# Tail of a decoder layer: TensorE transposes of the attention output replaced by transposing DMAs out of half-precision halves

## The reference, cut to what matters

```python
x = _layernorm(x + self_attention(x))                      # 16 batches of 112 tokens, D = 256
q, k, v = x @ Wq, ctx @ Wk, ctx @ Wv                       # 8 heads of 128; all 6000 keys seen by all 1792 tokens
out = softmax(1.5 * (q k^T) * DIM_HEAD ** -0.5 ...) @ v    # per head
x = _layernorm(x + out.reshape(1792, 1024) @ Wout + bout)
h = gelu(x @ ternary(W1).T + b1)                           # 1024 hidden
x = _layernorm(x + h @ ternary(W2).T + b2)
```

## Time and profile before

| | us |
|---|---|
| median of three runs | 2306.89 |
| the profiled execution | 2306.85 |
| its span in the profile | 2305.1 |
| around the span | 1.75 |

### The profile page before, as it was taken

The page is one execution under the profiler, slowest core; times in us unless marked ns, Lnnn a source line. Parts: engine busy times, 40 slices in busy tenths (PEclk is TensorE's granted clock), DMA queues, the critical chain, the costliest instruction groups (busy, mean ns, idle before and its releaser), DMA issues.

```text
span 2305.1 us, 61948 instructions
## 1 busy us (share of the span) xinstructions
PE 2252.5 (98%) x26078; PEld 1980.7 (86%) x26078; DVE 2020.4 (88%) x2241; ACT 1865.1 (81%) x2224; POOL 1898.6 (82%) x1153
## 2 busy tenths in 40 slices
PE   7998999999999999999999999999999999999998
PEld 4557998899889998899888998899889998998886
DVE  7878988988889888988898898988899888898876
ACT  4357888888888888888878888888888888888855
POOL 8675888888878888888888898888878888899953
PEclk8999999999999999999999999999999999999999
DMA  7400000000000000000000000000000000010220
GB/s 201 158 32 21 6 4 13 4 7 6 11 6 4 7 13 4 6 4 7 13 4 5 6 13 4 6 4 7 13 4 6 4 6 6 4 47 7 90 79 33
DMA packets 34837, 50.44 MB, mean 22 GB/s; under 512 B 2304, under 2 KB 27392, under 8 KB 34560
## 3 DMA queue, kind: packets, MB, share of 16 engines
q1 hardware_dynamic: 34560, 46.46, 6.5%
HBM read 30.99 MB, written 15.47 MB: 20 GB/s over the span
## 4 chain that ended last, share of the span: by engine, by line
PE 71%; POOL 15%; DVE 6%; issue 4%; ACT 3%; POOLq 0%; DVEq 0%; ACTq 0%
PE psum L420 26%; POOL e_lo L1618 12%; PE psum L452 9%; PE psum L445 9%; PE psum L450 5%; PE psum L448 5%; PE psum L567 4%; PE psum L557 4%; POOL e_hi L1612 3%; DVE run_max L1082 3%; ACT ring L847 2%; PE psum L693 2%; PE psum L740 1%; PE psum L529 1%; PE psum L574 1%
## 5 line engine op out<-in xcount | busy, mean ns | idle before, releaser
L1618 POOL TENSOR_TENSOR e_lo<-ring,e_hi 128x1024 f16<-128x1024 f32 (+1 forms) x665 | 1388.8, 2103 | 196.4 <-ACT ring L862 160.8
L1082 DVE TENSOR_TENSOR run_max<-psum,run_max 128x1024 f16<-128x1024 f32 (+1 forms) x616 | 737.9, 1198 | 183.5 <-ACT ring L847 180.3
L847 ACT ACTIVATE ring<-psum 128x1024 f32<-128x1024 f32 (+1 forms) x672 | 673.7, 1003 | 180.0 <-PE psum L420 104.8
L1103 DVE SCALAR_TENSOR_TENSOR ring<-ring,psum 128x1024 f32<-128x1024 f32 (+1 forms) x672 | 792.5, 1186 | 0.7 <-PE psum L660 0.7
L420 PE MATMUL psum<-qx_hi,k_hi 128*128 128x256 f16 x2632 | 718.0, 273 | 15.5 <-DVE run_max L1082 9.1
L420 PE MATMUL psum<-qx_hi,k_lo 128*128 128x256 f16 x2632 | 717.8, 273 | 0.0
L420 PE MATMUL psum<-qx_lo,k_hi 128*128 128x256 f16 x2632 | 717.7, 273 | 0.0
L452 PE MATMUL psum<-v_main,e_lo 128*128 128x129 f16 x4032 | 711.4, 220 | 0.0
L862 ACT ACTIVATE ring<-ring 128x1024 f32<-128x1024 f32 (+1 forms) x672 | 696.1, 1036 | 1.3 <-DVE ring L1103 0.7
L445 PE MATMUL psum<-v_main,e_hi 128*128 128x257 f16 x2016 | 550.4, 273 | 1.3 <-POOL e_lo L1618 1.3
L450 PE MATMUL psum<-v_main,e_hi 128*128 128x128 f16 x2016 | 446.9, 222 | 0.0
(11 more groups left out here) (203 smaller groups left out, 3171.2 us busy)
## 6 DMA issues: line engine op xcount, KB each, us to landing
o_scratch<-o_buf SPq DMA_DIRECT2D x56, 128.0 KB, 1.9
raw<-o_scratch SPq DMA_DIRECT2D x14, 512.0 KB, 4.4
stage<-in_ctxT SPq DMA_DIRECT2D x6, 500.0 KB, 3.9
stage<-in_ctxT SPq DMA_DIRECT2D x12, 250.0 KB, 4.9
w_scratch<-wall SPq DMA_DIRECT2D x1, 2304.0 KB, 10.9
wall<-w_scratch SPq DMA_DIRECT2D x6, 384.0 KB, 3.2
x<-in_xT SPq DMA_DIRECT2D x4, 448.0 KB, 6.6
res<-in_x SPq DMA_DIRECT2D x1, 1792.0 KB, 17.6
```

Source lines behind the costliest of these rows:

```text
L847: a.activation(ring[:, f % SLOTS, 0:n], pair(f)[:, 0:n], ACT.Copy).then_inc(s_kept, 1)
L1082: ins = v.tensor_tensor(run_max[:, 0:n], pair(f)[:, 0:n], run_max[:, 0:n], ALU.max)
L1103: v.scalar_tensor_tensor(slot, slot, LIFT, psum[:, 6, 0:QB].unsqueeze(1).broadcast_to([P, t, QB]), ALU.add, ALU.subtract).then_inc(s_sub, 1)
L1618: g.tensor_tensor(e_lo[f % NEL][:, 0:n], slot, e_hi[f % NEH][:, 0:n], ALU.subtract).then_inc(s_lo, 1)
```

## The change

A returned tile is no longer transposed by TensorE. ScalarE copies it from `raw` (SBUF) as float16 into the high part of `halved`, VectorE subtracts into the low part beside it (two buffers), and a transposing DMA on SyncE's queue (`turn_tile`) turns the 128 x 2048 float16 values (512 KB) into `oT`, which holds six tiles; TensorE's projection reads its operands there. `o_high(i)` waits for the load and, from tile 2 on, for the DMA of tile i - 2; `turn_tile(i)` waits for `o_low(i)` and, from tile 6 on, for the projection of tile i - 6. Eight tiles instead of five are split during the last groups, at every second turn from turn -1. The turns of the projections stay. The pairs of tiles 6 to 13 are projected into banks 6, 0, 1 and 6 instead of bank 6 alone, since banks 0 and 1 no longer receive transposes. On SyncE's queue the loads are spread out between the transposing DMAs.

```diff
-        O_TURN = {3 * i: i for i in range(5)}
+        O_TURN = {2 * i - 1: i for i in range(8)}
-        oT_hi = [at(KREG + 14336 + 2048 * r, f"oT_hi{r}", [P, NH, P], F16) for r in range(2)]
-        oT_lo = [at(KREG + 18432 + 2048 * r, f"oT_lo{r}", [P, NH, P], F16) for r in range(2)]
+        halved = [at(KREG + 14336 + 4096 * r, f"halved{r}", [P, NH, 2, DH], F16) for r in range(2)]
+        NOT = 6
+        oT = [at(CTX + 10240 + 4096 * r, f"oT{r}", [P, NH, 2, P], F16) for r in range(NOT)]
+        s_oT = [sem(f"t_turned{r}") for r in range(NOT)]
...
-            return (7, 3, 2)[p] if p < 3 else 6
+            return (7, 3, 2)[p] if p < 3 else (6, 0, 1)[p % 3]
-            return 6 if p == 5 else 7
+            return 0 if p == 5 else 7
...
-                def o_transposes(i):
...
                 def o_project(i, heads=range(NH)):
-                        pe.wait_ge(t_lo, i + 1)
+                        pe.wait_ge(s_oT[i % NOT], 16 * (i // NOT + 1))
...
+                        elif i == 2:
+                            pe.wait_ge(s_max, NF_ALL)
                         elif i == 6:
                             pe.wait_ge(s_sub, NF_ALL)
-                        elif i % 2 == 0 and p >= 4:
-                            pe.wait_ge(t_add, p)
+                        elif i == 12:
+                            pe.wait_ge(t_add, 4)
...
                 def o_high(i):
-                    a.wait_ge(t_tr, i + 1)
+                    a.wait_ge(s_raw[i % NRAW], 16 * (i // NRAW + 1))
                     if i >= 2:
-                        a.wait_ge(t_wp, i - 1)
-                    a.activation(oT_hi[i % 2]..., psum[:, 0:2, :], ACT.Copy).then_inc(t_hi, 1)
+                        a.wait_ge(s_oT[(i - 2) % NOT], 16 * ((i - 2) // NOT + 1))
+                    a.activation(halved[i % 2][:, :, 0, :], raw[i % NRAW][:, :, :], ACT.Copy).then_inc(t_hi, 1)
                 def o_low(i):
-                    v.tensor_tensor(oT_lo[i % 2]..., psum[:, 0:2, :], oT_hi[i % 2]..., ALU.subtract)
+                    v.tensor_tensor(halved[i % 2][:, :, 1, :], raw[i % NRAW][:, :, :], halved[i % 2][:, :, 0, :],
+                                    ALU.subtract).then_inc(t_lo, 1)
...
+                def turn_tile(i):
+                    sp.wait_ge(t_lo, i + 1)
+                    if i >= NOT:
+                        sp.wait_ge(t_wp, i - NOT + 1)
+                    sp.dma_start_transpose(oT[i % NOT][:, :, :, :].rearrange("p h x t -> p (h x) t"),
+                                           halved[i % 2][:, :, :, :].rearrange("p h x d -> p (h x d)")).then_inc(
+                                               s_oT[i % NOT], 16)
...
                     if n == NBLK - 3:
                         sp.wait_ge(s_lo, LATE)
-                        for i in range(3, 6):
+                        for i in range(3, 5):
                             load_tile(i)
+                        for i in range(3):
+                            turn_tile(i)
+                            load_tile(i + 5)
                     if n == NBLK - 2:
-                        for i in range(6, 10):
-                            load_tile(i)
-                for i in range(10, NTL):
-                    load_tile(i)
+                        for i in range(3, 7):
+                            turn_tile(i)
+                            load_tile(i + 5)
+                for i in range(7, NTL):
+                    if i + 5 < NTL:
+                        load_tile(i + 5)
+                    turn_tile(i)
```

More of the change, by code:

```diff
@@ L389, in columns @@
             return (FIRST[c + 1] - FIRST[c]) * P
-        (t_bias, t_tr, t_hi, t_lo, t_wp, t_n, t_cp, t_n3, t_add, t_nt, t_yh, t_yl, t_f1, t_ge, t_hh, t_hl, t_f2, t_add2,
+        (t_bias, t_hi, t_lo, t_wp, t_n, t_cp, t_n3, t_add, t_nt, t_yh, t_yl, t_f1, t_ge, t_hh, t_hl, t_f2, t_add2,
          t_bn, t_bn2, t_ag, t_sq, t_ag3, t_sq3, t_shift,
          t_n3a, t_last, t_out) = [
-            sem("t_" + n) for n in ("bias", "tr", "hi", "lo", "wp", "n", "cp", "n3", "add", "nt", "yh", "yl", "f1", "ge",
+            sem("t_" + n) for n in ("bias", "hi", "lo", "wp", "n", "cp", "n3", "add", "nt", "yh", "yl", "f1", "ge",
                                     "hh", "hl", "f2", "add2", "bn", "bn2", "ag", "sq", "ag3", "sq3", "shift", "n3a", "last",
@@ L684, in o_project @@
                             pe.wait_ge(s_late, 48)
+                        elif i == 2:
+                            pe.wait_ge(s_max, NF_ALL)
                         elif i == 6:
                             pe.wait_ge(s_sub, NF_ALL)
-                        elif i % 2 == 0 and p >= 4:
-                            pe.wait_ge(t_add, p)
+                        elif i == 12:
+                            pe.wait_ge(t_add, 4)
                     for h in heads:
-                        for n, (o, w) in enumerate(((oT_hi, wout_hi), (oT_hi, wout_lo), (oT_lo, wout_hi))):
+                        for n, (o, w) in enumerate(((0, wout_hi), (0, wout_lo), (1, wout_hi))):
                             mm = pe.matmul(psum[:, bank_of_projection(p), (i % 2) * D:(i % 2 + 1) * D],
-                                           lhsT=o[i % 2][:, h, :], rhs=w[:, h, :],
+                                           lhsT=oT[i % NOT][:, h, o, :], rhs=w[:, h, :],
                                            start=(h == 0 and n == 0), stop=(h == NH - 1 and n == 2))
@@ L770, in step @@
                         o_project(*O_PROJECT[turn])
-                    if turn in O_TURN:
-                        o_transposes(O_TURN[turn])
                 def blocks(first, last, past=0):
@@ L796, in _ @@
                 blocks((NH - 2) * NQB, NBLK)
-                o_transposes(5)
                 o_project(4)
-                o_transposes(6)
                 n_transposes(0)
                 o_project(5)
-                o_transposes(7)
                 n_transposes(1)
@@ L808, in _ @@
                     up(c, range(0, 4))
-                    o_transposes(i)
                     o_project(i - 1)
                     up(c, range(4, 8))
-                    o_transposes(i + 1)
                     o_project(i)
                     down(2 * c)
-                    if c == 0:
-                        o_transposes(i + 2)
                     n_transposes(2 * c + 2)
@@ L821, in _ @@
                         n_transposes(3)
-                        o_transposes(i + 3)
                         o_project(i + 2)
@@ L1032, in _ @@
                 a.wait_ge(s_bias, 16)
-                o_high(5)
                 second_root(0)
-                o_high(6)
                 n_high(0)
-                o_high(7)
                 n_high(1)
@@ L1437, in _ @@
                             inverse(3)
-                    if f - TAIL - 1 in O_TURN:
-                        o_low(O_TURN[f - TAIL - 1])
+                    if f - TAIL in O_TURN:
+                        o_low(O_TURN[f - TAIL])
                 first_residual(0)
@@ L1444, in _ @@
                 second_statistics(0)
-                o_low(5)
                 second_norms(0)
-                o_low(6)
                 n_low(0)
                 first_residual(2)
-                o_low(7)
                 n_low(1)
@@ L1676, in load_tile @@
                     if i >= NRAW:
-                        sp.wait_ge(t_tr, i - NRAW + 1)
+                        sp.wait_ge(t_lo, i - NRAW + 1)
                     sp.dma_start(raw[i % NRAW][:, :, :].rearrange("p h d -> p (h d)"),
                                  o_part[i * P:(i + 1) * P, :]).then_inc(s_raw[i % NRAW], 16)
+                def turn_tile(i):
[5 more added lines that the diff above has]
+                                               s_oT[i % NOT], 16)
                 for n in range(NBLK):
```

4 lines of the change are left out of this document (removed).

## The result

The changed kernel takes 2320.28 us in the median of four runs (2318.50 to 2320.63), the kernel before 2306.57 beside it: ratio 1.0057, 95% interval 1.0045 to 1.0070. By the ratio it is slower by 13.2 us (by the two medians 13.7) where 3.3 us gained were forecast; the time lies inside the range, near its upper end, but the side was wrong. The profiled execution after took 2318.50, the quickest of the four (span 2316.7 against 2305.1, so 11.6 more).

What follows compares the result with a forecast made beforehand. TensorE was taken to bound the kernel from turn 3 to the last projection. 1.5 (groups) + 7.8 (nine transpose blocks) - 1.2 (first norms) - 4.8 (DMA waits) = 3.3 us gained, from 2306.85 to 2303.5 us; range 2297 to 2321.

Steps and rivals of the forecast that it cites:

- 1.5 us gained in the groups: Last groups: four transpose blocks gone, 3.5 us, less some 1.4 lost to VectorE and 0.6 left for GpSimd; bounds 0 and 3.5.
- TensorE waits 1.2 us: Ahead of the first norms' transposes, behind the last group: TensorE waits 1.2 us for VectorE, including 0.1 for the queue.
- The 1.1 us credited for o_low(5): Road to the first norms: 4.8 us from the end of o_project(3), taken as 3.7 without o_low(5).
- A wait of 4.8 us for the DMA behind the groups: Projections of tiles 8 to 13: waits of 1.9, 1.4, 0.5 and 1.0 at tiles 8, 11, 12, 13.
- T: Time of one 512 KB transposing DMA from issue to landing: 4.2 us, the same for all 14, with 1.9 to 8.5 kept.
- TensorE's clock stays: Behind the groups: granted clock unchanged, since even 2280 to 2306, with 18.6 busy of 26 us, was granted 0.98.
- no wait at tiles 0 to 7: Projections of tiles 0 to 7: TensorE has no idle time there waiting for the transposing DMA.
- the 33 us behind the last projection: Stretch from the last projection's end to the span's end: hangs on that projection and keeps its length, 33 us.
- rival 2: Projections wait for the DMA, slower from T = 6.4 on; at T = 8, 13.6 us lost, 2320.5 us; chance 0.20.
- Rival 4: VectorE takes over as bound in all stages, gain 0 in the groups: 2305 to 2308; within the forecast's chance of 0.40.
- rival 3: The DMA's sixteen blocks pass one at a time: 30 us each, far over 2700, or near 2510 by 1309 ns; chance 0.05.

Runs made afterwards that it cites:

- Run 1: Changed kernel, but o_low of tiles 0 to 7 subtracts from PSUM banks instead of the SBUF tile (values not the reference's): 2312.94 us, 1.0022 of the kernel before.
- run 3: Changed kernel with a plain DMA of the same 512 KB in place of the transposing one, operands not transposed: 2315.76 us, 1.0036 of the kernel before.
- Run 6: Kernel before's TensorE transposes for tiles 0 to 3; tiles 4 to 13 by DMA, split earlier, DMA ahead of the load, Run 4's edit: 2303.64 us, 0.9988.
- Run 4: Changed kernel with ScalarE's wait for the bias moved ahead of the last output copies, so the root's table load starts earlier: 2319.95 us, 1.0055 of the kernel before.
- run 9: As run 8, but TensorE projects tile 5 before the first norms' transposes and tile 6 before those of tile 1: 2300.71 us, 0.9975 of the kernel before.
- run 2: Changed kernel with o_high and o_low of tiles 8 to 13 one place earlier in ScalarE's and VectorE's lists: 2309.59 us, 1.0010 of the kernel before.
- run 8: As Run 6, but TensorE transposes tile 4 too and tiles 5 and 6 are split in turns 10 to 12: 2303.05 us, 0.9983 of the kernel before.

## Why the prediction was wrong

**"1.5 us gained in the groups": wrong, 5.2 lost.** The step that failed is the allowance of 0.3 us per pair of turns for the mutual disturbance of VectorE and GpSimd, and the other 0.6 in all for GpSimd. The row was in sight: GpSimd's low half averaged 2.41 in that stretch against 2.13 for one undisturbed, and the prediction named the two SBUF inputs as the cause, but averaged the effect instead of asking what one instruction does to another. It is 0.97 us each time, on the cast too, and it filled GpSimd, 84% busy before in that stretch: 5.74 a pair for 4.8. Over the four pairs from 2184.18 to 2207.12 that is 3.7 us. The other 3.0 of the 6.7 fall at its start: o_low(0) took 2.26 us at 2174.89 instead of 1.1, and the low half of group 659 behind it 2.53; against turn 0 it ended 2.9 us later than before, where the prediction let it move by 0.3. TensorE waited 3.1 us for it (before, it waited 0.90 one turn later, for GpSimd), and some 3 us at half clock followed. Run 1 shows the cause: its groups take 36.05 us again. It also leaves the DMAs' traffic as it is, and run 3 rules the transposing out. Run 6, with one o_low in three turns out of PSUM and TensorE transposing, as before the change, has no such wait.

**"TensorE waits 1.2 us" at the first norms: wrong, 3.8.** Taking o_low(5) off the road was counted, but o_low(7) and its two waits, for the DMA that frees its buffer (1.67) and for GpSimd's lock, were put in its place, and the table load of 1.28 had lost its cover. The 1.1 us credited for o_low(5) was not there to be had: before, the root behind the table load ended at 2214.73 and VectorE went on at 2214.77, so o_low(5) had run beside the load. Another 1.2 us lie ahead of the second residual, which began 1.3 us behind the projection of tile 3 and 0.1 behind it before, and 0.9 lie between the start of L1308 and the reciprocal, half of it L1308's own; two norms took 0.35 less than counted. Run 4 prices the load's share at 0.8, run 9 shows that the road need not be short if TensorE has other work.

**"A wait of 4.8 us for the DMA behind the groups": the mechanism right, the size 7.8.** T was right (4.3 for 4.2). By tile, forecast and measured: 8: 1.9 and 3.5; 9 and 10: nothing and at most 0.2; 11: 1.4 and 1.4; 12: 0.5 and 0.5; 13: 1.0 and 2.5. At tiles 8 and 13 the DMA itself took 5.3 and 5.9 instead of 4.2; ahead of tile 8's stands the load of tile 13 on the same queue (0.4 later, and its traffic beside it). Why tile 13's took 5.9 with no load beside it was not settled: its traffic is over by 2279.3, after 2.9 us like that of tile 11, and the landing comes only at 2281.0, and run 1 has the same 5.9 there. That every one of these waits could be had for nothing by moving a split by one place (run 2) the prediction did not see, though it had written down which list position each split hung on.

**"TensorE's clock stays": wrong, and most of 3.8 us behind the groups.** The first norms' transposes 0.7 longer, the projection of tile 5 1.2, that of tile 8 1.6, and two more 0.2 each, these at full clock. It was argued from a stretch that was 72% busy but granted 0.98 in the mean; a mean over 26 us says nothing of the 3 us behind one long wait. With the 3.1 of the DMAs this makes 6.9 of the 7.0 us by which the third stretch missed.

**Right:** T in the median, and that it is the same for most tiles (4.2 was chosen between a load's 3.4 and a count of pieces, 4.7, with 1.9 to 8.5 left open, so that it came so near is partly luck); no wait at tiles 0 to 7; the 33 us behind the last projection (32.8). **Rivals:** the time given for rival 2 (2320.5) was met, but not its reason; T was 4.3 and not 8, and its price in the groups, o_high, o_low and T in a row, did not arise except for the one 1.67 us. Rival 2's threshold was also mis-worked: by the sum's own terms the waits reach the 8.1 us gained elsewhere at T = 5.3, not 6.4; with T at 4.3 nothing hung on it. That the time fell inside the range is luck: the range was drawn for a slow DMA. Rival 4, VectorE as the bound in all stages, was near the right idea but without GpSimd and without the losses: it allowed no more than a gain of nothing. Of rival 3, and of the Trainium skill's 1309 ns for one block ("VectorE: DVE Perf Modes", "The three transpose paths"): sixteen blocks in one DMA took 4.3 us, 0.27 each, so that price does not add up block by block. The estimate of 3.5 for T from the Trainium skill's "DMA: Bandwidth & Descriptors" ("Latency and other measured facts") was nearer, 0.8 short of the 4.3 measured.

## What to carry to other kernels

Before moving an elementwise operation from PSUM to SBUF, count the operands: with two of them in SBUF, VectorE and GpSimd worked one after the other here, and the sum of GpSimd's work and of these VectorE instructions (5.74 us a pair) has to fit the pitch, not each engine's own. A DMA in place of TensorE's work cost no wait behind the groups once its source was made one list place earlier; look for that place before weighing the DMA's latency. And a long wait of TensorE (2.0 to 3.9 us here) can be paid again in what follows, by 1.6 to 1.9 us at half clock, so fill it with work that is ready.

## What was new of the hardware

- VectorE's subtraction of 128 x 1024 with both inputs in SBUF took 1.2 us alone and 2.2 in the mean beside GpSimd, and held up the GpSimd instruction that it met by 0.97 to 0.99, the cast as much as the subtraction; with one input in PSUM it took 1.21, and the cast nothing more.
- A transposing DMA of 512 KB from SBUF to SBUF lands in 4.3 us (a plain one in 3.2) and holds the issuing queue for 2.0 of them (plain 0.47).
- TensorE's granted clock was 0.50 to 0.51 in the 3 us after idle times of 3.1, 3.5 and 3.8 us, and 0.58 in the mean of 4 us behind one of 2.0 (run 8), but 1.00 after one of 2.7 (run 6) and after one of 2.5 at tile 13, while the same 2.5 at tile 13 was followed by a slow projection in run 1. The length of the wait alone does not decide; what does was not tried and stays open. One such spell is 1.6 to 1.9 us, so differences of that size between single executions, run 1's spread among them perhaps, say little.
